# A masked graph-attention layer on one core: the column pieces of its first two row blocks take turns, and x is scaled in groups of four chunks

## What is computed

```python
s_i = emb @ attn[:d]
s_j = emb @ attn[d:]
e = leaky_relu(s_i + s_j.T, negative_slope=0.2)
e = e + where(adj > 0, 0.0, -1e9)
alpha = softmax(e, axis=1)
return _layernorm(x + alpha @ emb, axis=-1)
```

## Time and profile before

| | us |
|---|---|
| median of three timed runs | 256.71 (256.52 to 256.77) |
| the profiled execution's own time | 257.18 |
| its span, first to last instruction | 255.3 |
| TensorE busy | 242.9 (95%) |
| VectorE busy | 233.6 (91%) |
| ScalarE busy | 175.4 (69%) |
| GpSimd busy | 36.5 (14%) |

### The profile page before, as it was taken

One profiled execution on the slowest core, in us unless ns is written; L12 is line 12 of the kernel. 1 busy time (PEld: TensorE's weight loads), 2 busy tenths in 40 slices (PEclk: granted clock), 3 DMA queues, 4 the chain that ended last, 5 costly groups with the idle time before them and its releaser, 6 DMA issues.

```text
span 255.3 us, 2776 instructions
## 1 busy us (share of the span) xinstructions
PE 242.9 (95%) x801; PEld 127.9 (50%) x801; DVE 233.6 (91%) x383; ACT 175.4 (69%) x257; POOL 36.5 (14%) x76
## 2 busy tenths in 40 slices
PE   7998989989999999999999999999999999999980
PEld 6743434434444444444444444444444444899970
DVE  1979899989999999999999999999999999999552
ACT  0589999998499669495986579578965579204410
POOL 1000000000052003300430003300320004303322
PEclk9999999999999999999999999999999999999997
DMA  7999999999999999999999999999999940100101
GB/s 199 309 347 348 348 349 347 349 342 348 347 328 360 349 348 348 348 335 348 348 347 364 347 348 348 353 349 348 349 360 350 346 116 0 45 0 4 41 0 45
DMA packets 70227, 71.51 MB, mean 280 GB/s; under 512 B 2881, under 2 KB 68674, under 8 KB 70210
## 3 DMA queue, kind: packets, MB, share of 16 engines
q10 hardware_dynamic: 34592, 34.67, 43.5%
q1 hardware_dynamic: 34594, 34.67, 43.4%
q0 software_dynamic: 1024, 1.97, 2.5%
HBM read 69.21 MB, written 2.10 MB: 279 GB/s over the span
## 4 chain that ended last, share of the span: by engine, by line
PE 81%; ACT 6%; DMA 5%; issue 2%; ACTq 2%; SPq 1%; POOL 1%; DVE 1%
PE psum L866 69%; PE psum L870 11%; DMA adj_in<-in_adj_dram 5%; ACT xj L400 2%; ACTq L271 2%; ACT mask_bytes L412 2%; ACT mask_bytes L418 1%; PE psum L862 1%; SPq L253 1%; POOL out_dram L279 1%; ACT x_raw L503 0%; SPq L271 0%; DVE weights L721 0%; DVE x_raw L666 0%; SPq L292 0%
## 5 line engine op out<-in xcount | busy, mean ns | idle before, releaser
L866 PE MATMUL psum<-weights,xj 128*128 128x512 f32 x448 | 194.5, 593 | 2.9 <-ACT xj L400 2.0
L721 DVE SCALAR_TENSOR_TENSOR weights<-q_row,r_j,mask_t 128x512 f32<-128x512 f32 x256 | 172.2, 740 | 0.3
L866 PEld LDWEIGHTS psum<-weights,xj 128*128 128x128 f32 x448 | 84.0, 190 | 109.2 <-issue 82.2
L418 ACT ACTIVATE mask_bytes<-adj_in 128x4096 uint8<-128x4096 int32 x27 | 97.3, 3613 | 22.7 <-DMA adj_in<-in_adj_dram 15.2
L607 DVE STREAM_TRANSPOSE mask_t<-mask_bytes 128x1024 uint32<-128x1024 uint32 x27 | 33.4, 1236 | 0.9 <-ACT mask_bytes L418 0.9
L870 PEld LDWEIGHTS psum<-xj,weights 128*128 128x128 f32 x256 | 28.8, 192 | 0.5 <-issue 0.5
L870 PE MATMUL psum<-xj,weights 128*128 128x128 f32 x256 | 28.9, 275 | 0.0
L337 POOL TENSOR_SCALAR neg_mean<-total 128x4 f32<-128x4 f32 x7 | 1.6, 223 | 158.4 <-ACT x_raw L431 158.4
L431 ACT ACTIVATE x_raw<-x_raw 128x128 f32<-128x128 f32 x28 | 8.2, 295 | 15.3 <-DVE x_raw L666 15.3
L346 POOL DMA_DIRECT2D out_dram<-x_raw x28 | 14.6, 525 | 19.3 <-ACT x_raw L445 19.3
L412 ACT ACTIVATE mask_bytes<-adj_in 128x2048 uint8<-128x2048 int32 x9 | 17.0, 1901 | 0.0
(11 more groups left out here) (65 smaller groups left out, 81.7 us busy)
## 6 DMA issues: line engine op xcount, KB each, us to landing
adj_in<-in_adj_dram ACTq DMA_DIRECT2D x64, 512.0 KB, 13.0
adj_in<-in_adj_dram SPq DMA_DIRECT2D x64, 512.0 KB, 13.6
out_dram<-x_raw POOLq DMA_DIRECT2D x28, 64.0 KB, 5.3
x_raw<-in_x_dram ACTq DMA_DIRECT2D x4, 128.0 KB, 3.2
x_raw<-in_x_dram SPq DMA_DIRECT2D x4, 128.0 KB, 3.5
x_raw<-in_x_dram ACTq DMA_DIRECT2D x2, 256.0 KB, 6.1
x_raw<-in_x_dram SPq DMA_DIRECT2D x2, 256.0 KB, 7.0
out_dram<-x_raw POOLq DMA_DIRECT2D x4, 32.0 KB, 1.8
```

What stands on the lines that cost most here:

```text
L418: nc.scalar.activation(mask_bytes[:, g % BYTE_SLOTS, :, :, :], adj_in[:, g % ADJ_SLOTS, :, :, :], ACT.Sign).then_inc(bytes_ready, 1)
L721: nc.vector.scalar_tensor_tensor(weights[:, slot_of(n, c), :], q_row[:, n * BANK:(n + 1) * BANK], r_j[:, c:c + 1], mask_t[:, (n * PIECES + ...
L866: nc.tensor.matmul(banks[SUM_BANK[n % 2]][:, :], xj[:, c, :], weights[:, slot_of(n, c), :], start=(c == 0), stop=(c == CHUNKS - 1)).then_i ...
```

## The change

Up to now the pieces come block by block. In the changed kernel a list `ORDER` gives block and piece for each g: (block 0, piece 0), (1, 0), (0, 1), (1, 1), (0, 2), (1, 2), (0, 3), (1, 3), and then blocks 2 to 7 as before. Loads, masks, weights and products all follow it, each step's slot goes by its place in that order, and blocks 0 and 1 sum up in banks 3 and 2 at the same time. `END` says behind which g a block is complete: 7 for block 0 (it was 4), 8 for block 1 and so on as before.

With it change: the scaling of x, which now goes by four chunks behind each of pieces 1 to 6, all four behind both halves of the bytes; `q_piece(1)`, which moves ahead of the loop over g; the copy of block 0's sums, which moves from g = 4 to g = 7 and waits for 56 products instead of 32; block 0's turning back, from step 38 to step 62; and its residual, from step 51 to step 75. The same steps of block 1 stay at 70 and 83.

```diff
+    ORDER = [(n, p) for p in range(PIECES) for n in range(2)] + [(n, p) for n in range(2, BLOCKS) for p in range(PIECES)]
+    END = [max(g for g in range(ALL_PIECES) if ORDER[g][0] == n) + 1 for n in range(BLOCKS)]
...
-    TAKE_SUMS_AT = [4, 9, 13, 18, 22, 27, 31]
+    TAKE_SUMS_AT = [7, 9, 13, 18, 22, 27, 31]
...
+            n, p = ORDER[g]
             for q in quadrants:
                 queue.dma_start(adj_in[B * q:B * (q + 1), g % ADJ_SLOTS, :, :, :],
-                                adj_v[g // PIECES, g % PIECES, q, :, :, :, :]).then_inc(adj_loaded[g % ADJ_SLOTS], 16)
+                                adj_v[n, p, q, :, :, :, :]).then_inc(adj_loaded[g % ADJ_SLOTS], 16)
...
-                act.wait_ge(weights_used, (n + 1) * CHUNKS)
+                act.wait_ge(weights_used, END[n] * PC)
...
             scale_xj(3, PC)
+            q_piece(1)
             load_piece(act, HIGH_HALF[1:2], 3)
...
                     if g > BY_DVE:
                         load_piece(act, HIGH_HALF[1:2], g + 2)
-                    if g < PIECES:
-                        scale_xj(g * PC, g * PC + K)
                     half_to_bytes(g, 1)
                     load_piece(act, HIGH_HALF[0:1], g + 3)
-                    if g < PIECES:
-                        scale_xj(g * PC + K, g * PC + PC)
...
-                if g == PIECES - 1:
-                    q_piece(1)
-                elif g >= PIECES and 2 * (g - PIECES) + 2 < RB:
+                if PC + (g - 1) * K < CHUNKS:
+                    scale_xj(PC + (g - 1) * K, PC + g * K)
+                if g >= PIECES and 2 * (g - PIECES) + 2 < RB:
                     q_piece(2 * (g - PIECES) + 2)
                     q_piece(2 * (g - PIECES) + 3)
...
-            for n in range(BLOCKS):
-                dve.wait_ge(q_ready, n + 1)
-                for c in range(CHUNKS):
...
+            for g, (n, p) in enumerate(ORDER):
+                if p == 0:
+                    dve.wait_ge(q_ready, n + 1)
+                for j in range(PC):
...
+                    for m in range(BLOCKS - 1):
+                        if g * PC + j == END[m] * PC + RESIDUAL_AT:
+                            residual(m)
...
-                    if n > 0 and c == TURN_BACK_AT:
-                        turn_back(n - 1)
+                    for m in range(BLOCKS - 1):
+                        if g == END[m] and j == TURN_BACK_AT:
+                            turn_back(m)
```

More of the change, by code:

```diff
@@ L281, in store_last, with slot_of @@
                             ).then_inc(done, 16)
-        def slot_of(n, c):
-            return (n * CHUNKS + c) % W_SLOTS
+        def slot_of(step):
+            return step % W_SLOTS
         block = ctx.enter_context(nc.Block())
@@ L715, in final_residual, with weigh @@
                         last_normalise(g - 1)
-            def weigh(n, c):
-                if n * CHUNKS + c >= W_SLOTS:
-                    dve.wait_ge(weights_used, n * CHUNKS + c - W_SLOTS + 1)
+            def weigh(g, j):
+                n, p = ORDER[g]
+                c = p * PC + j
+                if g * PC + j >= W_SLOTS:
+                    dve.wait_ge(weights_used, g * PC + j - W_SLOTS + 1)
                 nc.vector.scalar_tensor_tensor(
-                    weights[:, slot_of(n, c), :], q_row[:, n * BANK:(n + 1) * BANK], r_j[:, c:c + 1],
-                    mask_t[:, (n * PIECES + c // PC) % MASK_SLOTS, c // K % PF, :, c % K],
+                    weights[:, slot_of(g * PC + j), :], q_row[:, n * BANK:(n + 1) * BANK], r_j[:, c:c + 1],
+                    mask_t[:, g % MASK_SLOTS, j // K, :, j % K],
                     ALU.max, ALU.min).then_inc(weights_ready, 1)
-            for n in range(BLOCKS):
-                dve.wait_ge(q_ready, n + 1)
-                for c in range(CHUNKS):
-                    g = n * PIECES + c // PC
-                    if c % PC == 0 and g in HALVED:
+            for g, (n, p) in enumerate(ORDER):
+                if p == 0:
+                    dve.wait_ge(q_ready, n + 1)
+                for j in range(PC):
+                    if j == 0 and g in HALVED:
                         dve.wait_ge(half_mask_ready, HALVED.index(g) + 1)
-                    elif c % PC == 0 or c % PC == K and g in HALVED:
+                    elif j == 0 or j == K and g in HALVED:
                         dve.wait_ge(mask_ready, g + 1)
[L734 to L737, removed]
+                    weigh(g, j)
+                    for m in range(BLOCKS - 1):
+                        if g * PC + j == END[m] * PC + RESIDUAL_AT:
+                            residual(m)
+                    if j == SECOND_HALF_AT and g in HALVED:
                         if g == 0:
@@ L743, in _ @@
                             turn_half(g, 1)
-                    if c % PC == (FIRST_TURN_AT if g == 0 else TURN_AT) and g + 1 < ALL_PIECES:
+                    if j == (FIRST_TURN_AT if g == 0 else TURN_AT) and g + 1 < ALL_PIECES:
                         if g + 1 < BY_DVE:
@@ L863, in turn_back, with block_product @@
                 last.then_inc(turned_back, 1)
-            def block_product(n, c):
-                nc.tensor.matmul(banks[SUM_BANK[n % 2]][:, :], xj[:, c, :], weights[:, slot_of(n, c), :],
+            def block_product(g, j):
+                n, p = ORDER[g]
+                c = p * PC + j
+                nc.tensor.matmul(banks[SUM_BANK[n % 2]][:, :], xj[:, c, :], weights[:, slot_of(g * PC + j), :],
                                  start=(c == 0), stop=(c == CHUNKS - 1)).then_inc(weights_used, 1)
             def product(c, t):
-                return nc.tensor.matmul(banks[((BLOCKS - 1) * K + t) % 8][:, 0:D], weights[:, slot_of(BLOCKS - 1, c), t * P:(t + 1) * P],
+                slot = slot_of((BLOCKS - 1) * CHUNKS + c)
+                return nc.tensor.matmul(banks[((BLOCKS - 1) * K + t) % 8][:, 0:D], weights[:, slot, t * P:(t + 1) * P],
                                         xj[:, c, :], start=(c == 0), stop=(c == CHUNKS - 1))
-            for n in range(BLOCKS):
-                last_chunks = LAST if n == BLOCKS - 1 else 0
-                for c in range(CHUNKS - last_chunks):
+            for g, (n, p) in enumerate(ORDER):
+                for j in range(PC):
+                    if g * PC + j >= ALL_PIECES * PC - LAST:
+                        continue
                     if n == 0:
-                        pe.wait_ge(xj_scaled, c + 1)
-                    pe.wait_ge(weights_ready, n * CHUNKS + c + 1)
-                    if c == 0:
+                        pe.wait_ge(xj_scaled, p * PC + j + 1)
+                    pe.wait_ge(weights_ready, g * PC + j + 1)
+                    if p == 0 and j == 0:
                         if n < 2:
@@ L887, in _ @@
                     if n < BLOCKS - 1:
-                        block_product(n, c)
+                        block_product(g, j)
                     else:
                         for t in range(K):
-                            last = product(c, t)
+                            last = product(p * PC + j, t)
                         last.then_inc(weights_used, 1)
-                    if n > 0 and c == TURN_BACK_AT:
-                        turn_back(n - 1)
+                    for m in range(BLOCKS - 1):
+                        if g == END[m] and j == TURN_BACK_AT:
+                            turn_back(m)
             for t in range(K):
```

## The result

| | before | changed |
|---|---|---|
| median, timed side by side | 256.41 us (20 runs) | 257.13 us (20 runs) |
| ratio, 95% interval | | 1.0028 (1.0017 to 1.0039) |
| profiled execution, its own time | 257.18 us | 256.91 us |
| its span | 255.3 us | 255.1 us |

The changed kernel is slower by a little, 0.28%; the forecast was 256.8 us and no change that can be told. Two things stand in this table that do not go together: by the medians 0.7 us are lost, by the two profiled executions 0.3 us are won. That is the question of the experiments.

A forecast was written before the change was run, and what follows sets the result against it. ScalarE was taken as the bound up to 57 us. Gains of 0.6 and 1.15 us against losses of 1.0 and 0.7 to 0.8, taken as +0.05 on the 256.71 median, gave 256.8 us; range 255.8 to 257.9.

The forecast's parts named there:

- (a): Scaling four chunks a piece instead of eight: ScalarE needs 5.15 us a piece against 6.0 between landings, so waits for landings.
- (c): Step 14: VectorE no longer waits at piece 2; TensorE starts at 33.4 instead of 33.98 us, 0.6 us won.
- (b): Block 1's exponentials ahead of piece 1's bytes: 0.57 us on ScalarE, uncovered; step 8 at 28.0 instead of 27.4 us.
- (d): Step 38 at 54.2 us, with piece 5's bytes there at 52.2 instead of 53.98; 1.74 us won by here.
- (e): Copy of block 0's sums, at 69.9 us, delays piece 8's bytes: a 1.1 us stop before step 62.
- (f): Residuals of blocks 0 and 1 in neighbouring pieces: new stop of 0.7 us, 0.8 with the restart, before step 86.
- Rival 1: Faster, hidden residuals: the stop at step 86 doesn't come; 256.0 us, chance 0.15.
- (g): After step 86: no further stop, and TensorE's 150 us to the end stay the same.
- Rival 2: Much faster: both old stops go and none comes for them; 253.8 to 255 us, chance 0.04.
- Rival 3: Slower, late bytes of piece 5 before step 38: 257.5 us at 1 us of delay, or 258.5; chance 0.17.
- Rival 4: Slower, clock at half speed while pieces take turns: 6.87 us for each piece, 263.6 us for one; chance 0.02.

The follow-up runs named there:

- the second comparison: The changed kernel, unaltered, timed once more beside the kernel before: 256.89 us, ratio 1.0006 (0.9989 to 1.0024).

## Why the forecast was nearly right, and where it failed

**(a) and (c), step 14: the mechanism holds.** ScalarE waits for landings, VectorE no longer waits at piece 2, and step 14 came 12.50 and 12.87 us after the first product; the forecast had 13.0. That VectorE's weights and not the scaling of x release TensorE, against the chain's word, is borne out by the old-scaling run, where the trace itself names the weights for a gap of 1.03 us at the same step; in the kernel before with two more instructions at its start, it names them for a gap of 1.13 us there.

**(b), the exponentials:** their price on ScalarE is as forecast: piece 1's bytes start 5.08 us after the scaling of chunk 1 in both traces of the changed kernel, and 4.50 to 4.51 us in both of the kernel before and in the run that moves them. At TensorE it was over-sized: step 8 came 7.19 and 7.33 us after the first product, against 7.03 and 6.95 before, so 0.2 to 0.4 us were lost there and not 0.57. Step 38 doesn't feel it in either place.

**(d), step 38: this step failed, in the size of its gain.** The forecast had 1.74 us: the 55.94 of before less 54.2. In the changed kernel 53.87, 54.05 and 54.09 were measured, so that end is right. The 55.94 was not typical: in that execution piece 0 landed at 17.45, the latest of all thirteen traces (16.12 to 17.45), and the load issue behind it took 1.85 us, and the kernel before hands on to step 38 what they cost the scaling of chunk 1: 1.10 us of difference at the scaling, 1.09 at step 38. Its time of 257.18 us is reached by only 3 of the 98 timed executions of the kernel before. In its second trace step 38 is at 54.85, and the gain is 0.8 us. The sum was made as one execution against itself and then put on the median as it stood. That holds if both kernels hang on the same event, and they do not: the one hangs on its start, the other on piece 4's landing, 25 us later. By the four profiled executions of the two unaltered kernels, 201.2 and 201.5 us pass from step 38 to the end of the program in the kernel before (257.18 less 55.94, 256.33 less 54.85), and 203.0 and 203.1 in the changed one (256.91 less 53.87, 257.12 less 54.05). The difference, 1.6 to 1.8 us, is the loss, and the forecast had 1.79. Less 0.8 us of gain it leaves 0.8 to 1.0 us slower, less the 2.07 of the first pair it leaves the 0.3 us faster that the two profiled executions show. The timed medians say 0.7 and 0.4 us, and the second comparison's ratio of 1.0006 says less still, 0.15 us; what the two comparisons' intervals have in common is 0.4 to 0.6 us. How the starts of the timed executions are spread was not measured; the 3 in 98 and the medians agree with mostly early ones, which is not shown.

That 256.8 lies so near to the measured 257.13 is in part luck. The forecast stood on 256.71, a median of three runs, and the median of twenty is 256.41; the change itself was forecast at 0.05 us and measured at 0.72. That is over the 0.5 us which the forecast called the least that can be told, and for a slower kernel it had named only late bytes of piece 5 and the clock, and neither was the cause.

**(e), the copy:** right in place and price. ScalarE waited at it until 69.59 (forecast 69.9), the gap before step 62 was 1.03 us, and moving the copy alone took it away, and in the kernel before took the gap before step 38 and 1.06 us away in the same manner. The load issues behind the wait go out at about 70 us as foretold, and cost the transfers something: 283 GB/s from 70 to 77 us, against 347 with the copy moved.

```profile
70.00:77.00 7.00, 5.97 (x16) 2.47 (x16) 4.42 (x7) 7.00 (x3) 0.00 (x0) 1.00 1.11 283
```

```profile
70.00:77.00 7.00, 7.00 (x21) 3.27 (x20) 7.00 (x11) 3.90 (x3) 0.00 (x0) 1.00 1.10 347
```

These are one stretch of the changed kernel and of the one with the copy moved (busy times by engine, granted clock, DMA share, GB/s). Nothing waited for it, since VectorE next waits for nothing but weights' slots and its own work.

**(f), the residuals:** right. 7.94 us twice, and a gap of 0.47 us (0.7 forecast) before step 86; what TensorE loses there is 0.7 us by its steps: from step 78 (90.4, 84.43 being step 71's start) to step 86 (98.03) it is 7.6 us instead of 6.87. Rival 1 is out, and the run with the residual at step 91 shows the cause.

**(g) and the other rivals.** No gap over 0.15 us comes after step 86 until the last block's end, where one of 2.08 us stands in the kernel before as well. (From step 86 to the end of the span it is 157 us, not the 150 that (g) has; nothing hangs on it.) Rival 2 is out: both later stops came. Rival 3, late bytes of piece 5, is true as a mechanism, one for one, but in the changed kernel's two traces piece 5 landed at 47.86 and 48.05 us, 0.3 us before ScalarE was free for it, which gave it no occasion. Rival 4, the clock: from 26 to 75 us, with a bank switch every eight steps, the changed kernel has a granted clock of 1.00, the 2.4 GHz level:

```profile
26.00:75.00 49.00, 48.03 (x111) 20.31 (x109) 45.44 (x67) 40.97 (x43) 0.00 (x0) 1.00 1.10 341
```

What the Trainium skill says in "TensorE: Matmul & The Clock Gate", section "A second HAM failure mode: psum-queue depth-cycling", of a clock that goes back and forth when banks are cycled does not occur here; in this stretch TensorE was busy for 48.03 of 49 us.

## What to carry to other kernels

A stop moves with the wait that makes it: before an order is changed, ask which copy or wait stands in front of the next piece's work on the same engine, and try that edit first; here it alone was worth 1.1 us in the old order and over 2 us in the new one. Before a difference of two schedules is put on a median, name the event from which each of them hangs, and look at more than one trace of the old kernel, above all when the profiled execution took longer than the timed ones (257.18 us against 256.71 here); an edit that removes a backlog also removes the gain of an early start. Deferred work that is moved next to its neighbour costs only what the engine's lead at that point doesn't cover.

## What the runs showed of the hardware that I had not expected

The start of one and the same kernel differs between executions: piece 0 landed at 17.45 and 16.71 us in the two traces of before, and in the thirteen traces, of kernels that hardly differ up to there, between 16.12 and 17.45 us. One transfer issue on ScalarE's queue behind it, of 512 KB, took 1.85 and 1.38 us. ScalarE stands still behind such an issue, 1.20 and 0.73 us here. An activation of 128 x 128 without a scale or bias from a tile took 0.20 us, where the scaling of 128 x 127 with both takes 0.385. The chain of waits named the scaling of x as what released TensorE in the kernel before, where only VectorE's weights fit in time and count.
